# Softmax sums inverted and maxima placed by VectorE transposes in a two-layer Perceiver kernel

## What is computed

```python
qh = _split_heads(q @ Wq.T)
kh = _split_heads(k @ Wk.T)
vh = _split_heads(v @ Wv.T)
scale = 1.0 / jnp.sqrt(jnp.asarray(HEAD_DIM, qh.dtype))
scores = jnp.einsum('bhqd,bhkd->bhqk', qh, kh) * scale
attn = jax.nn.softmax(scores, axis=-1)
out = jnp.einsum('bhqk,bhkd->bhqd', attn, vh)
...
return out @ Wo.T
```

## Time and profile before

| What | Value |
|---|---|
| Timed runs (3) | 1012.82, 1016.24 and 1017.31 us; median 1016.24 |
| Profiled execution, first to last instruction (span) | 1012.9 us |
| Busy: PE / PEld / DVE / ACT / POOL | 945.4 / 624.4 / 612.7 / 554.5 / 198.6 us |
| Rounds: first score matmul of round 0 | 54.3 us |
| Last weigh matmuls of round 15 | 723.1 us |

### The profile page before, as it was taken

How to read it: one execution, slowest core, us unless ns; L and a number is a source line. 1 busy time by engine, 2 the same in 40 slices (tenths; PEclk the granted TensorE clock), 3 DMA queues, 4 the chain that set the end, 5 groups by cost and what they waited for, 6 DMA issues and landing times.

```text
span 1012.9 us, 35591 instructions
## 1 busy us (share of the span) xinstructions
PE 945.4 (93%) x15476; PEld 624.4 (62%) x15476; DVE 612.7 (60%) x1022; ACT 554.5 (55%) x1056; POOL 198.6 (20%) x233
## 2 busy tenths in 40 slices
PE   5589889999999999999999999998899999999998
PEld 2256555656666665666666666666678544445887
DVE  6456656577476656758666786785774774435322
ACT  5368676677767767665666656756634622212200
POOL 4212112121211112121121221213446200000000
PEclk9789999999999999999999999999799999999999
DMA  8677484553635443444344345324211432232100
GB/s 303 192 225 224 114 260 125 160 167 90 194 89 155 129 109 89 120 116 127 88 132 137 94 118 137 83 54 152 85 57 33 163 125 83 83 125 83 43 1 22
DMA packets 70829, 123.79 MB, mean 122 GB/s; under 512 B 34770, under 2 KB 46082, under 8 KB 67412
## 3 DMA queue, kind: packets, MB, share of 16 engines
q1 hardware_dynamic: 69812, 119.84, 39.8%
q0 software_dynamic: 576, 1.35, 0.4%
q10 hardware_dynamic: 288, 0.33, 0.1%
HBM read 64.81 MB, written 17.32 MB: 81 GB/s over the span
## 4 chain that ended last, share of the span: by engine, by line
PE 74%; DVE 10%; ACT 7%; issue 4%; SPq 3%; POOL 2%; DMA 1%; ACTq 0%; POOLq 0%; DVEq 0%
PE ps L717 72%; DVE mpart L1366 3%; ACT p L1122 3%; SPq L472 3%; DVE rinv L1383 2%; PE ps L856 1%; DVE cl L1341 1%; POOL xg L658 1%; ACT ch L1080 1%; PE ps L886 1%; DMA qbscratch<-qb 1%; ACT k L1096 1%; ACT kh L1097 1%; DVE oT L1386 1%; ACT L1122 0%
## 5 line engine op out<-in xcount | busy, mean ns | idle before, releaser
L1366 DVE TENSOR_REDUCE mpart<-ps 128x2 f32<-128x800 f32 (+1 forms) x256 | 252.3, 988 | 140.8 <-PE ps L717 139.6
L1122 ACT ACTIVATE p<-ps 128x512 f32<-128x512 f32 (+1 forms) x416 | 225.4, 595 | 175.2 <-PE ps L717 173.9
L646 POOL TENSOR_TENSOR kl<-k,kh 128x400 f16<-128x400 f32 (+1 forms) x128 | 118.2, 925 | 450.0 <-ACT kh L1097 450.0
L717 PE MATMUL ps<-p,v 128*17 128x64 f32 x6656 | 133.1, 223 | 2.1 <-issue 2.1
L717 PEld LDWEIGHTS ps<-p,v 128*17 128x17 f32 x6656 | 98.9, 98 | 39.4 <-issue 37.4
L717 PE MATMUL ps<-wvh,ch 128*128 128x256 f16 (+1 forms) x416 | 115.1, 277 | 0.0
L717 PE MATMUL ps<-wvl,ch 128*128 128x256 f16 (+1 forms) x416 | 114.2, 275 | 0.0
L717 PE MATMUL ps<-wvh,cl 128*128 128x256 f16 (+1 forms) x416 | 114.2, 274 | 0.0
L717 PE MATMUL ps<-xcl,wh 128*128 128x512 f16 (+2 forms) x384 | 112.9, 308 | 0.0
L717 PE MATMUL ps<-xch,wh 128*128 128x512 f16 (+2 forms) x384 | 112.8, 308 | 0.0
L717 PE MATMUL ps<-xch,wl 128*128 128x512 f16 (+2 forms) x384 | 112.8, 308 | 0.0
(11 more groups left out here) (208 smaller groups left out, 1447.8 us busy)
## 6 DMA issues: line engine op xcount, KB each, us to landing
ks<-kh SPq DMA_DIRECT2D x256, 100.1 KB
w<-in_wgu SPq DMA_DIRECT2D x16, 1024.0 KB, 4.8
ks<-kl SPq DMA_DIRECT2D x128, 100.1 KB
w<-in_wd SPq DMA_DIRECT2D x8, 1024.0 KB, 4.8
c32a<-in_ctxT SPq DMA_DIRECT2D x16, 400.5 KB, 4.7
cparts<-ch SPq DMA_DIRECT2D x8, 800.5 KB, 6.2
cparts<-cl SPq DMA_DIRECT2D x8, 800.5 KB, 8.6
c32a<-in_ctxT SPq DMA_DIRECT2D x12, 400.0 KB, 3.2
```

Source lines behind the costliest of these rows:

```text
L646: nc.gpsimd.tensor_tensor(kl[:, mt, k0:k0 + w], k32[:, ku % 2, 0:w], kh[:, mt, k0:k0 + w], ALU.subtract).then_inc(sem("klo_done"), 1)
L717: return nc.tensor.matmul(o, lhsT, rhs, start=start, stop=stop, skip_group_check=shared)
L1122: nc.scalar.activation(p32[0:n, step % PRING, BANK * side:BANK * side + BANK], ps[0:n, side, :], ACT.Exp, scale=DH ** -0.5).then_inc(sem(" ...
L1366: nc.vector.reduce_max(mpart[:, j0:j0 + 3:2, quarter], o.rearrange("p (b c) -> p b c", b=2)[:, :, 0:w], AX.X).then_inc(sem("max_done"), 1)
```

## The change

**T.** There are no maxima matmuls and no ScalarE copies any more. VectorE writes minus m32 over 64 into every fourth column of m16 (now 128 x 32, zero elsewhere), transposes it in 32 x 32 blocks into mT, and copies mT, repeated 16 times, into qcur by `copy_predicated` where the constant mask `at` is one. The maximum of a pair of heads and half of the queries thereby lands on one of the partitions 4j that share a contraction; all of the constants in ks on partitions 4i are now 64.

**O.** There is no selection matmul, no copy and no osum. At the end of step 1 VectorE waits for the last weigh matmuls and does `divide(g - 1)` whole: it transposes pvb (256 columns) out of PSUM, takes the reciprocal of the 8 columns that hold sums, transposes them back spread over 32 partitions, and multiplies pvb with them into oT. `weigh(g, 0)` in step 3 now waits for oT_done.

Each step of these chains waits for the one before (`link`). The list of steps loses O; T no longer stands on TensorE or ScalarE. `sel` (64 KB) is no longer loaded, `at` (128 KB) is.

```diff
-              4: ["K4", "S", "P5", "W", "O"],
+              4: ["K4", "S", "P5", "W"],
...
-SUMS_STEP, DIVIDE_STEP = 2, 5
+SUMS_STEP = 1
...
-TAIL = ("x5 g O g x6 y5 g y6 g x7 g y7 h2 out x8 h3 g g g g g y8 s_norm s_turn l2 g s_u x9 g s_0 y9 x10 g s_1 y10 x11 g "
+TAIL = ("x5 g g x6 y5 g y6 g x7 g y7 h2 out x8 h3 g g g g g y8 s_norm s_turn l2 g s_u x9 g s_0 y9 x10 g s_1 y10 x11 g "
...
-        m16 = sb(ctx, "m16", [P, NP], F16)
-        rinv = sb(ctx, "rinv", [P, GROUPS, NQ])
-        osum = sb(ctx, "osum", [P, GROUPS, NQ])
+        m16 = sb(ctx, "m16", [P, SQUARE], F16)
+        mT = sb(ctx, "mT", [P, SQUARE], F16)
+        at = sb(ctx, "at", [P, NP, NQ], mybir.dt.uint16)
+        rinv = sb(ctx, "rinv", [P, GROUPS * NQ])
+        sumsT = sb(ctx, "sumsT", [P, GROUPS * NQ])
+        inverse = sb(ctx, "inverse", [P, GROUPS * NQ // SQUARE])
...
-            def t_unit(r, o):
-
-                if r == 0:
-                    pe.wait_ge(sem("const_ready"), 1)
-                pe.wait_ge(sem("m_ready"), r + 1)
-                for j in range(NP):
-                    last = mm(o[0:1, P * j:P * j + P], m16[:, j:j + 1], ident16[:, :], True, True)
-                last.then_inc(sem("t_mm"), 1)
-
-            def o_unit(r):
-
-                pe.wait_ge(sem("o_copied"), r + 1)
-                mm(mid[:, 0:GROUPS * NQ], sel[:, :], osum[:, :, :].rearrange("p g q -> p (g q)"), True,
-                   True).then_inc(sem("o_mm"), 1)
-
...
-                    pe.wait_ge(sem("qcur_in"), 16 * 3 * (g + 1))
+                    pe.wait_ge(sem(f"qcur_in{g % 2}"), 16 * 3 * (g // 2 + 1))
...
-                    need(pe, "o_copied", g)
+                    need(pe, "oT_done", g)
...
-                elif letter == "T":
-                    act.wait_ge(sem("t_mm"), r + 1)
-                    need(act, "main_mm", 2 * KT * (r - 1))
-                    act.wait_ge(sem("qcur_in"), 16 * 3 * (r + 1))
-                    for side in range(2):
-                        ins = nc.scalar.activation(qcur[r % 2][SIDE * side:SIDE * side + 1, :, :],
-                                                   o[0:1, :].rearrange("p (j s q) -> p s j q", j=NP, s=2)[:, side],
-                                                   ACT.Copy, scale=-1.0)
-                    ins.then_inc(sem("row_done"), 1)
...
                 elif letter == "T":
                     dve.wait_ge(sem("max_done"), 2 * NP * (r + 1))
-                    need(dve, "m_ready", r)
-                    nc.vector.reduce_max(m32[:, :], mpart[:, :, :], AX.X).then_inc(sem("m32_done"), 1)
-                    dve.wait_ge(sem("m32_done"), r + 1)
-                    need(dve, "t_mm", r)
-                    nc.vector.tensor_scalar(m16[:, :], m32[:, :], 1 / M_SCALE, None, ALU.mult)\
-                      .then_inc(sem("m_ready"), 1)
-
-            def divide(r, half):
-
-                two = slice(2 * half, 2 * half + 2)
-                dve.wait_ge(sem("o_mm"), r + 1)
+                    link(nc.vector.reduce_max(m32[:, :], mpart[:, :, :], AX.X))
+                    link(nc.vector.tensor_scalar(m16[:, 0:SQUARE:PARTS], m32[:, :], -1 / M_SCALE, None, ALU.mult))
+                    link(nc.vector.transpose(mT[:, :], m16[:, :]))
+                    if r == 0:
+                        dve.wait_ge(sem("at_in"), 16)
+                    need(dve, "main_mm", 2 * KT * (r - 1))
+                    dve.wait_ge(sem(f"qcur_in{r % 2}"), 16 * 3 * (r // 2 + 1))
+                    nc.vector.copy_predicated(qcur[r % 2][:, :, :].rearrange("p j (b q) -> p (j b) q", b=2),
+                                              at[:, :, :].rearrange("p j (b q) -> p (j b) q", b=2),
+                                              mT[:, :].unsqueeze(1).broadcast_to([P, 2 * NP, SQUARE]))\
+                      .then_inc(sem("row_done"), 1)
+
+            def divide(r):
+
+                dve.wait_ge(sem("pv_mm"), KT * (r + 1))
                 need(dve, "xo_mm", r // 2)
-                nc.vector.reciprocal(rinv[:, two, :], mid[:, 2 * NQ * half:2 * NQ * half + 2 * NQ]
-                                     .rearrange("p (g q) -> p g q", g=2)).then_inc(sem(f"o_inverse{half}"), 1)
-                dve.wait_ge(sem(f"o_inverse{half}"), r + 1)
-                nc.vector.tensor_tensor(oT[:, two, NQ * (r % 2):NQ * (r % 2) + NQ], osum[:, two, :],
-                                        rinv[:, two, :], ALU.mult).then_inc(sem("oT_done"), 1)
-
-            def take_sums(r):
-
-                dve.wait_ge(sem("pv_mm"), KT * (r + 1))
-                need(dve, "oT_done", 2 * r)
-                nc.vector.tensor_copy(osum[:, :, :], pvb).then_inc(sem("o_copied"), 1)
+                link(nc.vector.transpose(sumsT[:, :], ps[:, 2, 0:GROUPS * NQ]))
+                link(nc.vector.reciprocal(inverse[:, :], sumsT[:, DH:GROUPS * NQ:SQUARE]))
+                link(nc.vector.transpose(rinv[:, :], inverse[:, :].unsqueeze(2)
+                                         .broadcast_to([P, GROUPS * NQ // SQUARE, SQUARE])))
+                nc.vector.tensor_tensor(oT[:, :, NQ * (r % 2):NQ * (r % 2) + NQ], pvb,
+                                        rinv[:, :].rearrange("p (g q) -> p g q", g=GROUPS), ALU.mult)\
+                  .then_inc(sem("oT_done"), 1)
 
...
-                        if k == SUMS_STEP and name == "P2" and g:
-                            take_sums(g - 1)
-                    if k == DIVIDE_STEP and g:
-                        divide(g - 1, 1)
+                    if k == SUMS_STEP and g:
+                        divide(g - 1)
...
-            take_sums(G - 1)
+            divide(G - 1)
             for item in TAIL:
-                if item == "O":
-                    for half in range(2):
-                        divide(G - 1, half)
-                elif item[0] in "yl":
...
-    ones[:, 0] = M_SCALE
+    ones[:, :] = M_SCALE
     d["ones"] = ones.reshape(2 * DH, NP, S)
+    p, j, half = np.ogrid[0:P, 0:NP, 0:2]
+    place_of_max = (p % PARTS == 0) & (p % SQUARE // PARTS == j) & (p // SQUARE % 2 == half)
+    d["at"] = np.repeat(place_of_max, SQUARE, axis=2).astype(np.uint16)
```

More of the change, by code:

```diff
@@ L33 @@
 SIDE = 64
+SQUARE = 32
 PARTS = 4
@@ L171, in round_of @@
 def round_of(name, g):
-    return g + (0 if name in OWN_UNITS else {"O": -1, "N": 2}.get(name[0], 1))
+    return g + (0 if name in OWN_UNITS else (2 if name[0] == "N" else 1))
 def has_unit(name, g):
@@ L202, in read_by @@
     return {"K": ("khi_done", K_UNITS * r + i + 1), "N": ("khi_done", K_UNITS * r + i + 1),
-            "V": ("v_done", V_UNITS * r + i + 1), "P": ("max_done", 2 * NP * r + i + 1),
-            "T": ("row_done", r + 1), "O": ("oT_done", 2 * r + 2)}[name[0]]
+            "V": ("v_done", V_UNITS * r + i + 1), "P": ("max_done", 2 * NP * r + i + 1)}[name[0]]
 def event_read_by(name, layer, t):
@@ L224, in users_before @@
     for name in PROLOGUE_UNITS:
-        if name == "Q":
+        if name in ("Q", "T"):
             continue
@@ L233, in users_before @@
             for name in STEP_UNITS[k]:
-                if name in ("S", "W") or not has_unit(name, g):
+                if name in ("S", "W", "T") or not has_unit(name, g):
                     continue
-                r, at = round_of(name, g), 3 if name == "O" else place(name, False)
+                r, at = round_of(name, g), place(name, False)
                 before[name, r] = last.get(at)
@@ L242, in users_before @@
                     last[3] = event_read_by(*event)
-    before["O", G - 1] = last[3]
-    last[3] = read_by("O", G - 1)
     for event in LAST:
@@ L309, in build @@
         rows = sb(ctx, "rows", [P, 4, D])
-        sel = sb(ctx, "sel", [P, P])
         half = sb(ctx, "half", [P, 1])
@@ L681, in _ @@
             load(rows[:, :, :], d["rows"][:, 0:4, :], "const_in")
-            load(sel[:, :], d["sel"], "const_in")
             load(fb32[:, :], d["fb"], "const_in")
@@ L790, in run_unit @@
                 letter, i = name[0], int(name[1:] or 0)
-                o = None if letter == "O" else slot[place(name, prologue)]
+                o = None if letter == "T" else slot[place(name, prologue)]
                 if letter in "KN":
@@ L797, in run_unit @@
                     p_unit(r, i, o)
-                elif letter == "T":
-                    t_unit(r, o)
-                else:
-                    o_unit(r)
             def scores(g, k):
@@ L890, in event @@
                         pe.wait_ge(sem(f"wo{layer}_in"), 16)
-                    pe.wait_ge(sem("oT_done"), 2 * (B * layer + 2 * t + 2))
+                    pe.wait_ge(sem("oT_done"), B * layer + 2 * t + 2)
                     for e in range(GROUPS):
@@ L967, in _ @@
                     event("q_make", 0, 0)
-                else:
+                elif name != "T":
                     run_unit(name, int(name[0] == "N"), True)
-            pe.wait_ge(sem("const_in"), 80)
+            pe.wait_ge(sem("const_in"), 64)
             pe.wait_ge(sem("pv_clear"), 1)
@@ L974, in _ @@
                     for name in STEP_UNITS[k]:
```

(7 more changed lines are left out.)

18 lines of the change are left out of this document (6 added, 12 removed).

## The result

| | before | after |
|---|---|---|
| Median of 4 runs each on one chip | 1015.51 us (1012.82 to 1017.31) | 1000.3 us (997.97 to 1000.47) |
| Ratio after / before, 95% interval | | 0.9855 (0.9836 to 0.9875) |
| Span of the profiled execution | 1012.9 us | 998.3 us |
| First scores of round 0 to last scores of round 15 | 54.34 to 720.52 | 52.85 to 707.85 |

The kernel is 15.2 us (1.45%) faster; 999.0 was predicted, with a range of 991 to 1012. The span is 14.6 us shorter. Run once more, beside the last experiments, the changed kernel took 1001.67 us (ratio 0.9865, 0.9837 to 0.9894).

What follows compares the result with a forecast made beforehand. TensorE was taken as the bound, busy 945.4 of 1012.9 us. The terms 9.7 + 4.9 + 4.8 + 1.4 - 3.8 gave 17.0 us off the median of 1016.24: 999 us, range 991 to 1012.

Steps and rivals of the forecast that it cites:

- T: End of a round: matmuls leaving TensorE save 8.1 us, waits for m16 1.9, a new wait costs 0.3; net 9.7 us.
- The slack ahead of the first scores: End of round 6: masked copy done at 362.8, scores could start at 363.34, so 0.5 us to spare.
- Division: Steps 1 to 3: the division on VectorE, 1.55 us long, delays P3 in some rounds; costs 3.8 us together.
- the rule behind it: Steps 1 to 3: each microsecond of division beyond 1.55 delays P3 in 14 rounds, less some 4 us of slack.
- O in nine rounds: Steps 4 and 5: O's 0.54 us of TensorE counted in nine rounds only, 4.9 us; not in 2, 3, 5, 11, 13, 15.
- Tail: Behind the last O: a 0.86 us wait of transposes x7 and O's own 0.54 go, 1.4 us saved.
- O, what leaves TensorE: Steps 4 and 5: O takes 0.54 us a round off TensorE; counted in nine rounds, 4.9 us saved.
- O, what leaves VectorE: Reciprocals and products ahead of the maxima of P6 and P8 go; twelve waits at P7 and "out" vanish, 4.8 us saved.
- rival 2: Freed TensorE time is mostly given back at waits for VectorE and ScalarE: 9 or 10 us off, 1007 us; chance 0.16.
- The estimate of 0.31 to 0.62 us for a transpose: Division's transposes of 256 columns, from the skill's 311 ns for 128x128 bf16; whole sum then 15 to 18 us off.
- The first case: Whole kernel: the sum of the terms holds, 993 to 1004 us; chance 0.60.
- The third, the lock: Round's end: GpSimd's kl starts first and blocks VectorE's masked copy 0.75 us; costs 4.5 us, giving 1003; chance 0.06.

Runs made afterwards that it cites:

- T alone: Changed kernel with the maxima by transposes but the sums and their division as before, by the selection matmul: 1005.86 us against 1014.78, ratio 0.9912.
- the two runs: The changed kernel (1000.3 us), and the changed kernel with its masked copy run twice: 1011.38 us, ratio 0.9956.

## Why the prediction was right, and where not

**Right, term by term.** *T*: 9.7 predicted, 9.8 measured, in the whole change and alone. The slack ahead of the first scores was put at 0.5 us in round 6; the scores begin 0.6 us after the end of the copy in rounds 3, 5, 7 and 9, and only in round 15 do they wait for it (0.21 us). *Division*: 3.8 predicted, 3.4 measured, at the rounds named; P3 waits 1.25 in rounds 8 and 10 (1.4 predicted). Doubling the transposes showed that the rule behind it (D past the maximum of P1, one for one, less a slack) carries, to within a microsecond: 9.1 us by the formula, 8.4 measured beside the clock. *O in nine rounds*: rounds 11 and 13 gained 0.00 wherever the clock held, as said, and 1.0 once the gelu stood elsewhere. *Tail*: 1.4 predicted, 1.44 measured at the place.

**The mis-sized term.** The steps "O, what leaves TensorE" and "O, what leaves VectorE" promised 4.9 + 4.8 = 9.7, with the sentence "None of it returns". It was 7.3. By place, the first one failed: in the nine rounds that it counted, the scores of step 5 came only 1.4 us sooner and not 4.9. In seven of them TensorE now waits at K5 for ScalarE's kh, where it didn't. The second gave more than promised, 6.9 us in steps 6 and 7 of twelve rounds, of which 0.9 came back in steps 8 and 9 of rounds 3 and 5. K5's wait in round 8 is 0.41 us (timeline of PE, changed kernel):

```profile
415.16 0.34 PE L716 MATMUL ps<-ch,wkh 128*128 128x400 f16 x1 [0.41 <-ACT kh L1075]
```

The others have 0.22 to 0.59, 2.8 us in all. Round 8 gave 0.03 in step 5 where 0.54 was promised, and 0.96 in step 6 where 0.79 was: 0.99 together. That is rival 2 in small: I had looked at who else waits for VectorE, and not at who waits for ScalarE next.

**Not in the sum at all.** The clock in rounds 11 and 13 (+3.0 in this execution) and in round 15 (most of -1.4), the start with round 0 (-2.2) and the "issue" waits (+1.6, most of it in rounds 3 to 5). The start, round 15 and the "issue" waits are mostly not the change's: the kernel before with its gelu moved began its scores at 52.55 too, T alone, with xm still waited for, gained 1.3 of the 1.7 us in steps 10 to 12 of round 15, and the changed kernel's second profile is 2.7 us longer at the end of round 4, where the clock fell behind an "issue" wait of 1.13 us (granted clock 0.50 from 264 to 268) and in the first profile had not, behind one of 1.14. These terms cancel to within 1 us, so the closeness of 999.0 to 1000.3 is partly luck: the terms that could be worked out promised 17.0 and gave 15.6.

**Slips in the working.** The estimate of 0.31 to 0.62 us for a transpose put the sum between 15 and 18 us; one of 0.62 in place of 0.415 makes D 0.41 us longer, which by the prediction's own slacks costs some 3.5 us, so the lower end was 13.5. The lock's 13 x 0.25 + 2 x 0.75 is 4.75, not 4.5. Neither moves the forecast.

**The rivals.** The first case held. The third, the lock, I had at 0.06 as a cost; it costs nothing here, though the lock exists: the masked copy starts ahead of kl in every round that has one beside it, in round 6 by 0.57 us and at the end of round 11 by 0.04 us. The price went to GpSimd (kl takes 1.46 us there) and to a small scaling on VectorE, a_p, that now meets kl: 735 ns in place of 234. TensorE has no wait for either in the list. The changed kernel's timeline at the end of round 6:

```profile
355.34 0.69 DVE L1343 COPY_PREDICATED qcur<-at,mT 128x512 f16<-128x512 uint16 x1
...
356.14 0.75 DVE L1440 TENSOR_SCALAR a_p<-a_e,a_s 128x16 f32<-128x16 f32 x1
...
355.91 0.95 POOL L645 TENSOR_TENSOR kl<-k,kh 128x400 f16<-128x400 f32 x1 [2.46 <-ACT kh L1075]
```

The Trainium skill (SBUF — State Buffer, Who interferes with whom) says that issue order and not the shape of the operation decides who blocks; the two runs agree, 0.69 us where the copy starts first and 1.32 (the median) where it starts second.

## What to carry to other kernels

When an instruction leaves the engine that bounds a kernel, look not only at the waits that it causes but at the next instruction that waits for a *third* engine: a stall there takes the gain back (all of O's 0.54 us in rounds 11 and 13, part of it in seven others), and moving the cause of that stall may be worth more than the change. Of two operations that exclude each other, the order in which they start sets the price, so a margin of 0.04 us is a cost that hasn't come yet. And a sum that comes out right may hold two terms that cancel; compare intervals between fixed points of the program, and the granted clock in each, before calling it right or looking for the cause of a gain.
